# Layer norm rows split into fp16 parts before they are turned, and turned by transposing DMAs instead of TensorE

## The chip, the cores and the metric

One core of one Trainium2 chip runs the whole program. The metric is device time in microseconds (us). Engines are named as in the profile: PE is TensorE (PEld its weight loads), DVE is VectorE, ACT is ScalarE, POOL is GpSimd, SP is SyncE, which here only issues DMAs. PSUM is the memory that TensorE writes; SBUF is the other on-chip memory. The kernel is written by hand for each engine: an engine runs its own list of instructions in order, and waits on semaphores (counters) that others raise.

## The reference

```
x    = x + xattn(layernorm(x), ctx)          # x: 4 x 2048 x 512, ctx: 4 x 77 x 512
xattn: q = n @ Wq.T, k = ctx @ Wk.T, v = ctx @ Wv.T, 16 heads of 32
       a = softmax(mask(q k^T / sqrt(32))) v ;  return a @ Wo.T
x    = x + ffn(layernorm(x))
ffn:   s = n @ Win + bin (512 -> 64);  h = relu(s[..., None] * W1 + b1) (64 x 16)
       g = sum_h(h * W2) + b2 (64);    return g @ Wout + bout (64 -> 512)
```

All inputs are fp32. A product of two fp32 operands is made on TensorE from fp16 parts: each operand is split into a high part (rounded to fp16) and a low part (what is left), and three passes high·high, high·low, low·high are added up in PSUM (`three_passes`).

## The kernel before

The 8192 rows are 16 groups of 512 rows, each of 4 tiles of 128 rows. One step i of the pipeline works on several groups at once: it takes statistics of group i+2 ("ahead"), makes the normed rows and q of group i+1 ("front"), the logits and softmax of group i ("soft"), probabilities times v, the Wo product, the residual and the second norm of group i-1 ("back"), and the FFN of group i-2 ("ffn"). Steps run from -2 to 17; steps 2 to 13 are three rounds of a hardware loop over four steps. In each engine's `one_step` the order of the instructions is written out by hand, and it is that list that the diff rewrites.

A layer norm's output is needed with the 512 features on the partitions. Before: ACT (`x_normal`) or DVE (`h_normal`) writes the normed fp32 rows to `normed` (4 tiles), PE turns a tile by four 128x128 transposes into a bank of `tr_banks` (`x_transpose`, `h_transpose`), ACT copies the bank to the fp16 high part (`x_part`, `h_part`), and DVE subtracts that from the bank to make the low part (`x_low`, `h_low`), which also frees the bank.

The transposes of the probabilities (`p_transposes`, 16 heads, each copied out by ACT in `p_copies`) and the FFN's spreading products (`ffn_pre`, 8, each read by ACT in `relus`) use the same two banks `tr_banks` in turn (`TR_ORDER`): place n+2 waits for the reader of place n. The logits use two banks (`lg_banks`), of which each is freed by the first DVE instruction of `maxima`. A half k of a group's softmax goes PE `logits` -> DVE `maxima` -> POOL `subtract_max` -> ACT `exps` -> DVE `sums` -> POOL `divide`; the eight halves are 4 tiles x 2 halves of the heads. `p_transposes(step, 0)` waits until seven halves are divided, so on `divide(step, 6)`, which is the last instruction of POOL in the step before.

At the end of a step DVE runs, in this order, the statistics of the group ahead, `residual` of the four Wo tiles, the second norm (`h_means`, `h_normal`, `h_low`), with `q_low(3)` in between (the next step's `logits(0)` waits for it), and last `sums(step, 6)`. POOL runs `back_rstd`, `front_rstd`, four `add_bout` and the divisions 4 to 6 there. SP issues the loads of x, the stores of the output and the copies of k, and waits for each in order.

Of the kernel before, what the change touches and what calls it, by code (L numbers as in the profile page):

```python
# [31 lines left out]
F32 = mybir.dt.float32  # L32
F16 = mybir.dt.float16
# [6 lines left out]
P = 128  # L40
# [12 lines left out]
LW = HC * KEYS  # L53
HALVES = 2 * T
# [17 lines left out]
    [(FRONT, "xT", k) for k in range(0, 2)] + [(BACK, "pT", k) for k in range(0, 2)] + [(FFN, "pre", 0)]  # L72
    + [(BACK, "pT", 2)] + [(FFN, "pre", 1)] + [(BACK, "pT", k) for k in range(3, 5)]
    + [(FFN, "pre", k) for k in range(2, 4)] + [(BACK, "pT", 5)] + [(FFN, "pre", k) for k in range(4, 6)]
    + [(BACK, "pT", 6)] + [(FFN, "pre", k) for k in range(6, 8)] + [(BACK, "pT", 7)] + [(FRONT, "xT", 2)]
    + [(LATE, "wvT", k) for k in range(0, 4)] + [(BACK, "pT", k) for k in range(8, 12)] + [(FRONT, "xT", 3)]
    + [(BACK, "pT", k) for k in range(12, 15)] + [(LATE, "woT", k) for k in range(0, 2)] + [(BACK, "pT", 15)]
    + [(LATE, "woT", k) for k in range(2, 4)] + [(BACK, "hT", k) for k in range(0, 4)]
# [46 lines left out]
class Ring:  # L125
# [41 lines left out]

    def wait_all_read(self, eng, step):

        for b in range(2):  # L170
            eng.wait_ge(self.free[b], self.half(step))
# [6 lines left out]
def build(nc, x, ctx_in, mask, Wq, Wk, Wv, Wo, Win, bin_, W1, b1, W2, b2, Wout, bout, out):  # L178
    stack = ExitStack()
    with stack:  # L180
# [41 lines left out]
        pT = sb("pT", [P, 8, ROWS], F32)  # L222
# [18 lines left out]
        wvT = pT[:, 4:8, :]  # L241
# [7 lines left out]
        mask_raw = normed[:, :, 0:T * KEYS].bitcast(I32)  # L249
# [33 lines left out]
        x_high = sem("x_high")  # L283
        q_high = sem("q_high")
# [14 lines left out]
        h_high = sem("h_high")  # L299
        s_high = sem("s_high")  # L300
# [23 lines left out]
        def _(sp):  # L324
# [31 lines left out]


# [18 lines left out]

            sp.wait_ge(wout_high, 1)
# [13 lines left out]
            with sp.Fori(0, LOOPED // 4, 1) as t:  # L391
                for v in range(FIRST_FULL, FIRST_FULL + 4):
                    step = Step(t, v)
                    if v % 2 == 0:
                        sp.wait_ge(lg_ready, HALVES * step.i)
                        keys(0 if v % 4 == 2 else 1, t + 1)
                    for half in range(2):
                        store(step, half)

                        sp.wait_ge(out_stored[step.group(2).slot][half], 16 * step.group(2).lap)  # L400
                        load(step.group(2), (half,))
            for i in range(FIRST_FULL + LOOPED, GROUPS + 2):
                for half in range(2):
                    store(Step(0, i), half)
# [114 lines left out]
        def _(act):  # L519
# [53 lines left out]
            def x_normal(g, t):  # L573

                act.wait_ge(x_shift, g.n + 1)
                act.activation(normed[:, t, :], xr[:, g.slot, t, :], ACT.Identity, scale=rstd[:, 0, t:t + 1],
                               bias=shift[:, t:t + 1]).then_inc(x_norm, 1)

            def x_part(step, t):
                tr.wait_ready(act, step, "xT", t)  # L580
                act.activation(xT[:, 0, :, P * t:P * (t + 1)], tr.bank(step, "xT", t).rearrange(
                    "p (c r) -> p c r", c=C), ACT.Copy).then_inc(x_high, 1)

            def h_part(step, t):
                tr.wait_ready(act, step, "hT", t)
                act.activation(hT[:, 0, :, P * t:P * (t + 1)], tr.bank(step, "hT", t).rearrange(  # L586
                    "p (c r) -> p c r", c=C), ACT.Copy).then_inc(h_high, 1)
# [725 lines left out]
```

## Time and profile before

| | us |
|---|---|
| Three runs of the kernel | 977.37, 977.57, 981.69 (median 977.57) |
| Span of the profiled execution | 976.4 |
| PE busy | 890.4 (91%) |
| DVE busy | 743.7 (76%) |
| ACT busy | 529.9 (54%) |
| POOL busy | 445.5 (46%) |

The span is the profiled execution's own time, from its first to its last instruction. A busy time is the time in which an engine ran at least one instruction. A row of a timeline gives the start, how long the instruction or the run of like instructions lasted, the engine, the line of the kernel, the output and the inputs, and in brackets how long the engine had been idle and for whom it waited. A step begins, for the reading here, where the Wo product (L1054 with `woT`, x48) starts on PE.

### The profile page before, as it was taken

What the parts mean: (1) busy time and instruction counts of PE and PEld (TensorE: products, weight loads), DVE (VectorE), ACT (ScalarE), POOL (GpSimd) and SP (SyncE); (2) the same over time, 40 slices, a digit from 0 to 9 for tenths busy, and PEclk for the clock granted to TensorE, in tenths of its full rate; (3) what the DMA queues carried; (4) which work ended last, traced back from release to release, by engine and by line L of the source; (5) the groups of instructions that cost most, each with busy time, mean ns of one, the idle gap of its engine ahead of it and who ended that gap; (6) DMA issues with size and microseconds to landing.
All of it is one profiled execution on the core that took longest, in us unless ns stands there. A gap on an engine that the chain in (4) does not pass through costs nothing.

```text
span 976.4 us, 15372 instructions
## 1 busy us (share of the span) xinstructions
PE 890.4 (91%) x5202; PEld 478.6 (49%) x5202; DVE 743.7 (76%) x1338; ACT 529.9 (54%) x897; POOL 445.5 (46%) x398
## 2 busy tenths in 40 slices
PE   6878799999999989999999989999999999997866
PEld 4434545454555545454555545454555545453331
DVE  2446888888979796888979786888979798778351
ACT  2334638475574837475574827475574738273622
POOL 4033445364636453364646453364645454455220
PEclk9799899999999999999999999999999999999997
DMA  9300000202020110202020110202020100001001
GB/s 341 96 1 0 13 1 7 88 1 87 7 74 21 61 33 4 87 1 87 7 87 8 65 30 3 87 1 87 7 88 7 66 21 35 10 1 44 4 40 44
DMA packets 23314, 42.77 MB, mean 44 GB/s; under 512 B 11519, under 2 KB 12183, under 8 KB 23231
## 3 DMA queue, kind: packets, MB, share of 16 engines
q1 hardware_dynamic: 22303, 40.44, 12.4%
q10 hardware_dynamic: 928, 1.27, 0.4%
q8 instruction: 46, 0.75, 0.3%
q14 instruction: 37, 0.30, 0.1%
HBM read 22.90 MB, written 16.78 MB: 41 GB/s over the span
## 4 chain that ended last, share of the span: by engine, by line
PE 60%; DVE 18%; issue 9%; ACT 7%; POOL 5%; ACTq 0%; DVEq 0%; POOLq 0%
PE mm_banks L1054 19%; PE tr_banks L1105 12%; PE lg_banks L1094 8%; PE mm_banks L1116 7%; DVE normed L862 4%; PE mm_banks L1159 3%; ACT inner L618 3%; DVE xr L846 3%; PE tr_banks L1063 3%; PE mm_banks L1170 3%; DVE row_sum L833 2%; PE tr_banks L1151 2%; DVE stats L787 2%; ACT pT L603 2%; PE tr_banks L1136 2%
## 5 line engine op out<-in xcount | busy, mean ns | idle before, releaser
L468 POOL TENSOR_TENSOR probs<-probs,row_max 128x616 f32<-128x616 f32 x128 | 154.4, 1217 | 181.8 <-DVE row_max L825 181.0
L475 POOL TENSOR_TENSOR probs<-probs,row_inv 128x616 f32<-128x616 f32 x128 | 156.6, 1224 | 154.9 <-DVE row_inv L835 154.9
L1054 PE MATMUL mm_banks<-xT,wqT 128*128 128x512 f16 x768 | 177.4, 382 | 1.5 <-DVE xT L800 1.5
L1054 PE MATMUL mm_banks<-woT,aT 128*128 128x512 f16 x768 | 168.4, 379 | 2.1 <-issue 2.1
L1105 PE MATMUL tr_banks<-ident,probs 128*77 128x128 f32 x1024 | 155.7, 282 | 15.0 <-ACT inner L618 6.1
L1105 PEld LDWEIGHTS tr_banks<-ident,probs 128*77 128x77 f32 x1024 | 117.5, 148 | 95.1 <-issue 34.5
L603 ACT ACTIVATE pT<-tr_banks 77x512 f32<-77x512 f32 x256 | 145.7, 589 | 20.5 <-PE tr_banks L1105 18.2
L1094 PE MATMUL lg_banks<-k_blocks,qT 128*128 128x308 f16 x768 | 125.2, 300 | 15.4 <-issue 12.6
L833 DVE TENSOR_REDUCE row_sum<-probs 128x8 f32<-128x616 f32 x128 | 100.3, 784 | 46.2 <-ACT probs L598 45.2
L586 ACT ACTIVATE hT<-tr_banks 128x512 f16<-128x512 f32 x64 | 34.8, 594 | 171.5 <-PE tr_banks L1136 171.5
L1054 PEld LDWEIGHTS mm_banks<-woT,aT 128*128 128x128 f16 x768 | 75.1, 98 | 93.3 <-issue 3.2
L1054 PEld LDWEIGHTS mm_banks<-xT,wqT 128*128 128x128 f16 x768 | 75.5, 98 | 81.8 <-issue 3.1
L821 DVE TENSOR_TENSOR probs<-lg_banks,mask_bias 128x616 f32<-128x616 f32 x128 | 101.0, 789 | 9.7 <-PE lg_banks L1094 4.6
L825 DVE TENSOR_REDUCE row_max<-probs 128x8 f32<-128x616 f32 x128 | 101.8, 795 | 4.4
L1094 PEld LDWEIGHTS lg_banks<-k_blocks,qT 128*128 128x128 f16 x768 | 72.3, 99 | 62.8 <-issue 29.3
L618 ACT ACTIVATE inner<-tr_banks,inner_cols,w_div 128x512 f32<-128x512 f32 x128 | 95.5, 772 | 10.9 <-PE tr_banks L1151 10.9
L591 ACT ACTIVATE qT<-mm_banks 128x512 f16<-128x512 f32 x64 | 38.2, 597 | 109.2 <-PE mm_banks L1054 109.2
L598 ACT ACTIVATE probs<-probs 128x616 f32<-128x616 f32 x128 | 90.7, 710 | 5.4 <-POOL probs L468 3.5
L457 POOL TENSOR_TENSOR xr<-xr,bout_rows 128x512 f32<-128x512 f32 x64 | 85.6, 1338 | 9.8 <-DVE normed L862 9.8
L447 POOL TENSOR_TENSOR rstd<-var_eps,neg_half 128x2 f32<-128x2 f32 x32 | 22.6, 708 | 117.5 <-DVE var_eps L857 116.1
L1116 PE MATMUL mm_banks<-pT,v_now 77*32 77x512 f32 x512 | 68.2, 604 | 1.8 <-issue 1.7
L806 DVE TENSOR_TENSOR qT<-mm_banks,qT 128x512 f16<-128x512 f32 x64 | 43.9, 686 | 32.2 <-ACT qT L591 31.7
(80 smaller groups left out, 1055.5 us busy)
## 6 DMA issues: line engine op xcount, KB each, us to landing
xr<-in_x SPq DMA_DIRECT2D x32, 512.0 KB, 4.6
out_x<-xr SPq DMA_DIRECT2D x32, 512.0 KB, 2.8
k_blocks<-kT_all SPq DMA_DIRECT2D x32, 38.5 KB, 2.2
probs<-in_L_xattn_Wk SPq DMA_DIRECT2D x1, 1024.0 KB, 8.7
probs<-in_L_xattn_Wq SPq DMA_DIRECT2D x1, 1024.0 KB, 12.8
probs<-in_L_xattn_Wv SPq DMA_DIRECT2D x1, 1024.0 KB, 14.4
probs<-in_L_xattn_Wo SPq DMA_DIRECT2D x1, 1024.0 KB, 16.2
xr<-in_ctx SPq DMA_DIRECT2D x1, 616.0 KB
```

Source lines behind the costliest of these rows:

```text
L468: pool.tensor_tensor(block_of(g, k), block_of(g, k), top, ALU.subtract).then_inc(shifted, 1)
L475: pool.tensor_tensor(block_of(g, k), block_of(g, k), inv, ALU.mult).then_inc(probs_ready, 1)
L598: act.activation(p, p, ACT.Exp, scale=DK ** -0.5 / W_SCALE).then_inc(exp_done, 1)
L603: tr.read(act.activation(pT[0:KEYS, h % 8, :], tr.bank(step, "pT", h)[0:KEYS, :], ACT.Copy), step, "pT", h)
L618: tr.read(act.activation(inner[:, j, :], tr.bank(step, "pre", j), ACT.Relu, bias=inner_cols[:, 1, j:j + 1], scale=w1_div[:, j:j + 1]), ste ...
L821: dve.tensor_tensor(probs_of(g, k), logits_of(k), mask_bias[:, g.slot, k // 2, :].unsqueeze(1).unsqueeze(1).broadcast_to([P, 2, HC, KEYS]) ...
L825: dve.tensor_reduce(row_max[:, g.parity, k, :, :], probs_of(g, k), AX.X, ALU.max)\
L833: dve.tensor_reduce(row_sum[:, k % 2, :, :], p, AX.X, ALU.add).then_inc(sum_done, 1)
L1054: last = pe.matmul(bank, stationary(a, c), moving(b, c), start=(n == 0), stop=(n == len(passes) - 1))
L1094: last = pe.matmul(bank, qT[:, g.parity, qp, c, rows], k_blocks[:, buffer, kp, c, :], start=(m == 0), stop=(m == 2))
L1105: last = pe.transpose(tr.bank(step, "pT", h)[0:KEYS, P * t:P * (t + 1)], probs[:, g.parity, t, KEYS * h:KEYS * (h + 1)], ident[:, :])
L1116: last = pe.matmul(mm.bank(step, "pv", c)[DK * h:DK * (h + 1), :], v_now[:, DK * (HC * c + h):DK * (HC * c + h + 1)], pT[0:KEYS, (HC * c + ...
```

## The change

The normed rows are split in row layout. `normed` shrinks from four tiles to two, shared in turn by both norms. ACT copies a tile of `normed` to the fp16 high part in a new buffer `parts`, DVE subtracts `parts` from `normed` for the low part, and SP issues one transposing DMA for each tile, which turns both parts at once (8 blocks of 128x128 fp16) from `parts` into `xT` or `hT`. PE no longer turns these rows; `q` and `ffn_in` wait for the DMAs. `parts` has four tiles for both norms: the first norm's tile t of a step is written only when the DMA of the second norm's tile t of the step before has landed, and the other way round. `pT` shrinks from 8 to 6 slots. SP's loop is unrolled.

```diff
-        normed = sb("normed", [P, T, D], F32)
-        xT = sb("xT", [P, 2, C, ROWS], F16)
-        hT = sb("hT", [P, 2, C, ROWS], F16)
+        normed = sb("normed", [P, 2, D], F32)
+        parts = sb("parts", [P, T, 2, D], F16)
+        xT = sb("xT", [P, T, 2, C, P], F16)
+        hT = sb("hT", [P, T, 2, C, P], F16)
...
+            def turn_x(step, t):
+                g = step.group(1)
+                if t == 0 and not step.first(-1):
+                    mm.wait_all_ready(sp, step)
+                sp.wait_ge(x_low_done, 4 * g.n + t + 1)
+                sp.dma_start_transpose(xT[:, t, :, :, :].rearrange("p a c r -> p (a c) r"),
+                                       parts[:, t, :, :].rearrange("p a d -> p (a d)")).then_inc(x_turned[t], 16)
+
+            def turn_h(step, t):
+                g = step.group(-1)
+                if t == 0 and not step.first(1):
+                    mm.wait_ready(sp, step, "s", 0)
+                sp.wait_ge(h_low_done, 4 * g.n + t + 1)
+                sp.dma_start_transpose(hT[:, t, :, :, :].rearrange("p a c r -> p (a c) r"),
+                                       parts[:, t, :, :].rearrange("p a d -> p (a d)")).then_inc(h_turned[t], 16)
...
+                for k in range(T):
+                    turn_x(step, k)
+                for half in range(2):
+                    store(step, half)
+
+                    sp.wait_ge(out_stored[step.group(2).slot][half], 16 * step.group(2).lap)
+                    load(step.group(2), (half,))
+                for k in range(T):
+                    turn_h(step, k)
...
             def x_part(step, t):
-                tr.wait_ready(act, step, "xT", t)
-                act.activation(xT[:, 0, :, P * t:P * (t + 1)], tr.bank(step, "xT", t).rearrange(
-                    "p (c r) -> p c r", c=C), ACT.Copy).then_inc(x_high, 1)
+                g = step.group(1)
+                if not (step.first(-1) or step.first(0) or step.first(1)):
+                    act.wait_ge(h_turned[t], 16 * (g.n - 2))
+                elif not step.first(-1):
+                    act.wait_ge(x_turned[t], 16 * g.n)
+                act.wait_ge(x_norm, 4 * g.n + t + 1)
+                act.activation(parts[:, t, 0, :], normed[:, t % 2, :], ACT.Copy).then_inc(x_high, 1)
...
             def h_low(step, t):
                 dve.wait_ge(h_high, 4 * step.group(-1).n + t + 1)
-                rows = slice(P * t, P * (t + 1))
-                tr.read(dve.tensor_tensor(hT[:, 1, :, rows], tr.bank(step, "hT", t).rearrange("p (c r) -> p c r", c=C),
-                                          hT[:, 0, :, rows], ALU.subtract), step, "hT", t)
+                dve.tensor_tensor(parts[:, t, 1, :], normed[:, t % 2, :], parts[:, t, 0, :], ALU.subtract)\
+                    .then_inc(h_low_done, 1)
...
             def ffn_in(step):
 
-                tr.wait_all_read(pe, step)
+                for t in range(T):
+                    pe.wait_ge(h_turned[t], 16 * (step.group(-2).n + 1))
```

`x_normal` and `h_normal` of tiles 2 and 3 now wait for the low part of tiles 0 and 1 (two tiles of `normed`). On DVE `x_low(2)` and `x_low(3)` move up among the first `maxima`, and `s_low` moves behind `x_low(3)`.

PE, from the end of one step of the loop to the FFN's part of the next, before. L1136 and L1063 are the transposes of the second and the first norm, L1094 the logits, L1105 the probabilities' transposes, L1054 with `hT` is `ffn_in`, L1151 is `ffn_pre`.

```order
L1094 MATMUL lg_banks<-k_blocks,qT 128x308 x6
...
L1136 MATMUL tr_banks<-ident,normed 128x128 x4
...
L1094 MATMUL lg_banks<-k_blocks,qT 128x308 x6
...
L1063 MATMUL tr_banks<-ident,normed 128x128 x4
L1061 REGISTER_ALU
L1063 MATMUL tr_banks<-ident,normed 128x128 x4
L1054 MATMUL mm_banks<-hT,win 128x512 x12
...
L1105 MATMUL tr_banks<-ident,probs 77x128 x8
L1094 MATMUL lg_banks<-k_blocks,qT 128x308 x6
...
L1151 MATMUL tr_banks<-s_parts,spread 128x512
```

The same place of the changed kernel (L1145 logits, L1156 the probabilities' transposes, L1114 with `hT` is `ffn_in`, L1195 is `ffn_pre`):

```order
L1145 MATMUL lg_banks<-k_blocks,qT 128x308 x6
...
L1145 MATMUL lg_banks<-k_blocks,qT 128x308 x6
L1152 REGISTER_ALU
L156 ISA
L1156 MATMUL tr_banks<-ident,probs 77x128 x8
L1145 MATMUL lg_banks<-k_blocks,qT 128x308 x6
...
L1156 MATMUL tr_banks<-ident,probs 77x128 x4
...
L1156 MATMUL tr_banks<-ident,probs 77x128 x4
L1186 REGISTER_ALU
L1114 MATMUL mm_banks<-hT,win 128x512 x12
L165 REGISTER_ALU
L1195 MATMUL tr_banks<-s_parts,spread 128x512
```

The transposes of both norms are gone, the probabilities' transposes stand right behind `logits(0)`, and `ffn_in` stands behind those of head 4, with `ffn_pre(0)` directly after it.

ACT at the start of a step, before (L576 `x_normal`, L581 `x_part`, L612 `s_part`, L603 `p_copies`, L618 `relus`):

```order
L576 ACTIVATE normed<-xr,shift,rstd 128x512 x2
L161 ISA
L581 ACTIVATE xT<-tr_banks 128x4x128
L161 REGISTER_ALU
L581 ACTIVATE xT<-tr_banks 128x4x128
L576 ACTIVATE normed<-xr,shift,rstd 128x512
L161 ISA
L612 ACTIVATE s_parts<-mm_banks,bin 128x512
L161 REGISTER_ALU
L603 ACTIVATE pT<-tr_banks 77x512
```

and now (L626 `x_normal`, L636 `x_part`, L658 `p_copies`, L667 `s_part`):

```order
L626 ACTIVATE normed<-xr,shift,rstd 128x512 x2
L160 ISA
L658 ACTIVATE pT<-tr_banks 77x512
...
L635 REGISTER_ALU
L636 ACTIVATE parts<-normed 128x512
L160 REGISTER_ALU
L658 ACTIVATE pT<-tr_banks 77x512
...
L658 ACTIVATE pT<-tr_banks 77x512
L160 ISA
L667 ACTIVATE s_parts<-mm_banks,bin 128x512
L160 REGISTER_ALU
L673 ACTIVATE inner<-tr_banks,inner_cols,w_div 128x512
```

`s_part`, and with it all eight `relus`, come behind the copies of heads 0 to 4, and two `x_part` stand among these copies.

## Rows read from the trace of the kernel before

**Rows 1.** The page, section 4: shares of the chain that ended last.

```profile
PE 60%; DVE 18%; issue 9%; ACT 7%; POOL 5%; ACTq 0%; DVEq 0%; POOLq 0%
```

**Rows 2.** Busy time by stretch: start:end, length, each engine (x instructions), clock, DMA, GB/s.

```profile
405.47:459.05 53.58, 51.97 (x318) 28.05 (x317) 45.63 (x83) 31.91 (x54) 27.21 (x25) 1.00 0.13 40
405.47:426.72 21.25, 20.47 (x110) 10.69 (x108) 20.18 (x44) 7.86 (x13) 14.33 (x14) 1.00 0.00 0
426.72:441.40 14.68, 13.85 (x100) 8.12 (x100) 11.64 (x17) 12.82 (x21) 4.21 (x4) 1.00 0.01 2
441.40:459.05 17.65, 17.65 (x111) 9.24 (x112) 13.80 (x24) 11.23 (x20) 8.67 (x8) 1.00 0.37 120
```

**Rows 3.** Timeline of PE: start, us, what, [idle before, releaser].

```profile
405.47 10.52 PE L1054 MATMUL mm_banks<-woT,aT 128*128 128x512 f16 x48
...
420.90 1.11 PE L1136 MATMUL tr_banks<-ident,normed 128*128 128x128 f32 x8 [0.65 <-DVE normed L862]
422.13 0.96 PE L1094 MATMUL lg_banks<-k_blocks,qT 128*128 128x308 f16 x6
...
424.13 2.75 PE L1054 MATMUL mm_banks<-hT,win 128*128 128x512 f16 x12
```

**Rows 4.** Groups of instructions, PE: both norms' transposes; busy, mean ns, idle before.

```profile
L1063 PE MATMUL tr_banks<-ident,normed 128*128 128x128 f32 x256 | 41.7, 295 | 3.0 <-ACT normed L576 2.1 <-DVE xT L800 0.6
L1136 PE MATMUL tr_banks<-ident,normed 128*128 128x128 f32 x256 | 34.9, 281 | 17.3 <-DVE normed L862 17.3
```

**Rows 5.** Timeline of DVE in the second norm.

```profile
417.49 0.69 DVE L868 TENSOR_TENSOR hT<-tr_banks,hT 128x512 f16<-128x512 f32 x1
419.36 1.94 DVE L862 TENSOR_SCALAR normed<-xr,mean_var,rstd 128x512 f32<-128x512 f32 x2 [0.23 <-POOL rstd L447]
421.22 0.68 DVE L806 TENSOR_TENSOR qT<-mm_banks,qT 128x512 f16<-128x512 f32 x1
```

**Rows 6.** Timeline of POOL over the same time.

```profile
417.29 1.22 POOL L475 TENSOR_TENSOR probs<-probs,row_inv 128x616 f32<-128x616 f32 x1
...
419.29 1.27 POOL L457 TENSOR_TENSOR xr<-xr,bout_rows 128x512 f32<-128x512 f32 x1
...
424.79 1.22 POOL L475 TENSOR_TENSOR probs<-probs,row_inv 128x616 f32<-128x616 f32 x1
```

**Rows 7.** Timeline of DVE and POOL while FFN weights are split.

```profile
98.13 0.78 DVE L764 SCALAR_TENSOR_TENSOR inner<-inner 64x512 f16<-64x512 f32 x1 [1.05 <-ACT inner L559]
98.33 2.27 POOL L475 TENSOR_TENSOR probs<-probs,row_inv 128x616 f32<-128x616 f32 x1
98.84 0.68 DVE L767 SCALAR_TENSOR_TENSOR win<-inner,win 128x512 f16<-128x512 f32 x1
```

**Rows 8.** Timelines of ACT and DVE at the FFN's first product.

```profile
426.92 0.69 ACT L612 ACTIVATE s_parts<-mm_banks,bin 128x512 f16<-128x512 f32 x1 [1.16 <-PE mm_banks L1054]
...
427.64 0.76 DVE L874 SCALAR_TENSOR_TENSOR s_parts<-mm_banks,bin,s_parts 64x512 f16<-64x512 f32 x1 [0.47 <-ACT s_parts L612]
```

**Rows 9.** Timeline of ACT: two `relus`, one of `exps`, one of `p_copies`.

```profile
434.53 1.43 ACT L618 ACTIVATE inner<-tr_banks,inner_cols,w_div 128x512 f32<-128x512 f32 x2
435.86 0.71 ACT L598 ACTIVATE probs<-probs 128x616 f32<-128x616 f32 x1
436.70 0.59 ACT L603 ACTIVATE pT<-tr_banks 77x512 f32<-77x512 f32 x1
```

**Rows 10.** The page, section 6: DMA issues, KB of each, median us to landing.

```profile
k_blocks<-kT_all SPq DMA_DIRECT2D x32, 38.5 KB, 2.2
...
probs<-in_L_xattn_Wo SPq DMA_DIRECT2D x1, 1024.0 KB, 16.2
```

**Rows 11.** Timeline of PE: the Wo products of steps 5, 15 and 16.

```profile
346.98 10.52 PE L1054 MATMUL mm_banks<-woT,aT 128*128 128x512 f16 x48
...
886.21 10.52 PE L1054 MATMUL mm_banks<-woT,aT 128*128 128x512 f16 x48 [0.58 <-issue]
933.52 10.52 PE L1054 MATMUL mm_banks<-woT,aT 128*128 128x512 f16 x48 [1.48 <-issue]
```

More of the change, by code:

```diff
@@ L166, in wait_read, with wait_all_ready @@
         eng.wait_ge(self.free[place % 2], self.half(step) + place // 2 + 1)
+    def wait_all_ready(self, eng, step):
+        eng.wait_ge(self.ready, 2 * self.half(step))
     def wait_all_read(self, eng, step):
@@ L389, in store @@
                 sp.dma_start(out_rows[g.n][:, tiles, :], xr[:, g.slot, tiles, :]).then_inc(out_stored[g.slot][half], 16)
[L391 to L401, printed above, removed]
+            for k in range(T):
+                turn_x(Step(0, 1), k)
+            for k in range(T):
+                turn_h(Step(0, 1), k)
+            for i in range(FIRST_FULL, FIRST_FULL + LOOPED):
+                step = Step(0, i)
+                if i % 2 == 0:
+                    sp.wait_ge(lg_ready, HALVES * i)
+                    keys(0 if i % 4 == 2 else 1, (i - FIRST_FULL) // 4 + 1)
+                for k in range(T):
+                    turn_x(step, k)
[3 more added lines that the diff above has]
+                    load(step.group(2), (half,))
+                for k in range(T):
+                    turn_h(step, k)
             for i in range(FIRST_FULL + LOOPED, GROUPS + 2):
+                step = Step(0, i)
+                if FRONT in step.parts:
+                    for k in range(T):
+                        turn_x(step, k)
                 for half in range(2):
-                    store(Step(0, i), half)
+                    store(step, half)
+                if BACK in step.parts:
+                    for k in range(T):
+                        turn_h(step, k)
             for s in range(4):
@@ L650, in one_step @@
                 if ffn:
+                    s_part(step)
+                    relus(step, 0)
+                if back:
+                    p_copies(step, 5)
+                if ffn:
+                    relus(step, 1)
                     relus(step, 2)
+                if back:
+                    exps(step, -1)
+                    p_copies(step, 6)
+                if ffn:
                     relus(step, 3)
                 if back:
-                    p_copies(step, 5)
+                    a_part(step, 0)
                 if ffn:
@@ L658, in one_step @@
                 if back:
-                    exps(step, -1)
-                    p_copies(step, 6)
+                    p_copies(step, 7)
                 if ffn:
@@ L663, in one_step @@
                     relus(step, 7)
-                if back:
-                    a_part(step, 0)
-                    p_copies(step, 7)
-                if front:
-                    x_part(step, 2)
                 if late:
@@ L681, in one_step @@
                     p_copies(step, 9, 10, 11)
-                if front:
-                    x_part(step, 3)
                 if late:
@@ L726, in one_step @@
                     q_part(step, 3)
-                if ahead:
-                    x_normal(step.group(2), 0)
                 if back:
@@ L732, in one_step @@
                 if ahead:
+                    x_normal(step.group(2), 0)
                     x_normal(step.group(2), 1)
@@ L902, in one_step @@
                     x_low(step, 1)
+                if soft:
+                    maxima(step, 0)
+                    maxima(step, 1)
+                if front:
+                    x_low(step, 2)
+                if soft:
+                    maxima(step, 2)
+                if front:
+                    x_low(step, 3)
                 if ffn:
@@ L915, in one_step @@
                     a_low(step, 0)
-                if front:
-                    x_low(step, 2)
                 if soft:
@@ L927, in one_step @@
                     output(step, 2)
-                if front:
-                    x_low(step, 3)
                 if ffn:
```

132 lines of the change are left out of this document (57 added, 75 removed).

## The prediction

> **What bounds the kernel now.** I read the shares of the chain first: PE holds 60% of it, DVE, ACT and POOL together 30% [rows 1]. That says PE is the bound with the others close behind, and it is an average, so I cut one step of the loop out. From one first Wo product to the next it takes 53.58 us, PE is busy 51.97 of them and DVE 45.63 [rows 2]. Cut again, the step has three stretches. In the first, 21.25 us from the Wo product to the first transpose of probabilities (call it pT0), DVE is busy 20.18 us and POOL 14.33 us: nearly as full as PE's 20.47. In the second, 14.68 us up to the end of the FFN's g product, ACT is busy 12.82 us. Only the third, 17.65 us, is PE alone (17.65) [rows 2]. So a microsecond taken from PE is worth a microsecond only in the third stretch.
>
> All times in a step below are counted from its Wo product, T = 405.47 in the trace [rows 3].
>
> **What is removed.** The 512 transposes cost PE 41.7 + 34.9 = 76.6 us of busy time and 17.3 + 3.0 us of waits before them, 96.9 us over 16 groups, about 6.1 us a group [rows 4]. Of the 32 transposes of a step, 24 lie in the first stretch, 8 in the other two, at about 0.16 us (41.7/256) each: 1.3 us outside the first stretch.
>
> **First stretch: where the gain goes.** Without the transposes and with `ffn_in` moved behind, PE has four Wo products, q(3) and two logits to do before pT0. Four Wo products end at T+10.4 (10.52 less the overlap), q(3) takes 2.6 as `ffn_in` does (426.72 - 424.13) and each logits 0.9 (423.06 - 422.13 is the slot) [rows 3]: PE is there at T+14.8. But pT0 waits for `divide(step, 6)` on POOL, which runs from 424.79 for 1.22 us, to T+20.5 [rows 6]. Before, pT0 stood at T+21.25, so this chain was hidden by 0.7 us only. It does not go through PE once the Wo products are done: DVE residuals, the POOL and DVE work of the norm, q_low(3) at 421.22 (for which `logits(0)` waits, which began at 422.13 before), then `sums(6)`, then POOL [rows 3, 5, 6]. Nothing of it is shortened. The gain of the first stretch is 0.7 us and PE idles for almost 6.
>
> **The lock, first stretch.** The new `h_low` and `x_low` read two SBUF operands (`normed`, `parts`); the old ones read PSUM and SBUF [rows 5]. The trace has such DVE instructions once: L764 and L767, back to back from 98.13 to 99.5. A POOL division that started at 98.33 took 2.27 us instead of 1.22, so 1.05 us more, about what was left of the two [rows 6, 7]. In the second norm there is the same seen from DVE: `h_normal` x2 starting 0.07 us after an `add_bout` takes 1.94 us [rows 5, 6], where two alone take 1.0. I take it that the new low parts and POOL's big instructions exclude each other. The Trainium skill says the same (SBUF — State Buffer, "Who interferes with whom": a DVE instruction with two SBUF inputs and a GpSimd one that reads SBUF block each other for a whole instruction); the trace agrees with its 2.27 us. Worked through the step: h_low(0), at 417.49, finds the division of 417.29 running [rows 5, 6] and starts some 0.9 us later, and with it the variance of the second pair, its rstd, h_normal(2) and (3). h_low(2) and (3) then hold POOL for another 2 x 0.6. Together +2.0 us on `divide(6)`: pT0 at T+22.6. Bounds: 0 if there is no such lock, 3.1 if POOL keeps it through its run of three instructions and DVE waits for all.
>
> **Second stretch.** ACT must now do, in its order, four `x_normal` and `x_part`, of which `x_normal(2)` and `(3)` wait for `x_low(0)` and `(1)`. I place these: without the lock head 0 is copied at T+22.1, with it at T+24.6, since x_low(0) and (1) stand behind POOL's last division and hold it. Then heads 1, 2 and two `x_part` follow at 0.54 us each, head 4's transposes end at T+27.4, `ffn_in` (2.6) at T+30.0. Here comes a wait that had a cover before: `s_part` 0.69 and `s_low` 0.76 [rows 8], with 0.15 for signals 1.6 us, lay beside pT0, pT1 and logits(1), and now `ffn_pre(0)` stands directly behind `ffn_in`. It starts at T+31.7. From there ACT is the bound: eight `relus` at 0.7, three `p_copies` at 0.54, one `exps` 0.62 and one `a_part` 0.54 (spacings of the rows) are 8.4 us [rows 9], with two banks in turn and PE's own order 9.3 until g can start. g takes 1.9, end at T+42.9. Before it was at 441.40, T+35.9: +7.0.
>
> **Third stretch.** PE alone as before, less one tile of transposes (4 x 0.16, with the overlap 0.44): 17.2. The step is 42.9 + 17.2 = 60.1 us, +6.5.
>
> **The DMAs.** Eight transposing DMAs of 256 KB a step. No row shows one. Below: 2.2 us, the small SBUF copy; above: 16.2 us, the slowest landing shown [rows 10]. I take 3, near the lower row, as plain SBUF traffic of a quarter of the size of the upper row's, whose 16.2 us include others ahead of it. Below even 2.2, nothing changes. With 3 the last `h_low` at T+19 lands at T+23.5 at the latest, `ffn_in` needs it at T+27.4, and `x_part(3)` at T+26.8: hidden, by 3 us. SP has nothing else there: its stores and loads come mid-step, behind four `turn_x` that are ready by T+33 and before any output. From about 5 us apiece the cover is gone (`x_part(3)` waits, and ACT's copies behind it, and PE for them), from 60.1/8 = 7.5 us SP's DMAs bound the step.
>
> **Sum.** Steps 2 to 14 are 13 full ones: 13 x 6.5 = 84.5. Step 15 has no first norm: +7.1 (0 off for x, the rest as above). Step 16 has no softmax of its own, which leaves `ffn_in` moved, s uncovered and part of the lock: +3.0 on 47.3 us [rows 11]. The last step gets the DMA's latency and the lock: +2.7. Three rounds of the loop cost 58.49 - 53.58 = 4.9 us where engines start a new round (346.98 to 405.47, [rows 2, 3, 11]); PE's share now falls into its wait for POOL: -1.7 each, -5.1, estimated from the 4.9 less what DVE alone would lose. The setup: four tiles go through a DMA before the first q, +2.5, and steps 0 and 1 save their transposes, -2.5. Together +92, on a span of 976.4: 1068.6. The median of the runs shown is 1.2 above the span: 1070.
>
> **Rivals.**
> The same without the lock. pT0 at T+20.6, head 0 copied at T+22.1, `ffn_pre(0)` at T+29.3, g ends at T+40.4: 57.6 a step, 13 x 4.05 = 53, end +8.6, rounds -5: 976.4 + 57 + 1.2, about 1034. For it: the evidence for two SBUF inputs is one division. Against: its 1.05 us fits well.
> Only the first wait. If ACT and PE pack the second stretch as tightly as before, `ffn_in` 2.6 and s 1.6 are added, the 6.6 us of the first stretch's transposes and `ffn_in` are lost to the wait: T+20.6 + 16.5 + 17.2 = 54.3 a step, 13 x 0.75 = 10, with the ends 985 to 995. Against it: ACT is busy 12.82 of 14.68 us there already [rows 2].
> Faster. PE stays the bound because POOL's division of the seventh half comes earlier than I think, the DVE queue in front of it being shorter by its waits for PE's transposes. It decides from a division that ends by T+14.8; then 76.6 us of transposes and some of their waits go, less 6 for the setup and the end: about 900. For it: PE is 91% busy. Against: DVE has 20.18 busy of 21.25 us there, only 0.23 us of a wait before h_normal [rows 2, 5].
> The DMAs are slow. At 10 us each SP needs 80 us a step: 13 x 26.4 on top, about 1320; at 6 us some 9 us a step and 1100 to 1190. For it: nothing in the trace; against: the small copy's 2.2 us [rows 10]. The Trainium skill has both answers: 1309 ns for one 128x128 block (VectorE: DVE Perf Modes, "The three transpose paths"), of which a DMA here has eight, and "TRN2 transpose DMAs are as fast as regular DMAs" (Advanced Engine Details and Errata, "X-Bar Transpose (TRN2)"). By the first, if blocks don't overlap, this rival is the outcome, by the second the cover holds; no run here shows it yet.
>
> **How the numbers follow.** The forecast 0.46 (1045 to 1095, by the lock's bounds); no lock 0.23 (1015 to 1045); only the first wait 0.08 (978 to 1000); faster 0.12; slow DMAs 0.11 (from 1100 up). The range 978 to 1125 leaves out the faster case, most of the slow DMAs and a little of the forecast's own tail, 0.2 together. A measurement tells 0.5%, 5 us, from no change: faster 0.12 and a trace of the third case 0.01, within 0.05 from the third case and chance, slower 0.82.
>
> **What would show it.** In the changed profile: PE idle 5 to 8 us a step before L1156 at a step's start, released by POOL's division (right: first stretch); an idle of 1.6 us before L1195, released by DVE `s_parts`; PE's transposes of probabilities and `ffn_pre` waiting for ACT; POOL divisions or `add_bout` of 1.8 us and more, or low parts of 1.2 and more, in the second norm (right: lock; all at 1.2 and 0.69: wrong); transposing DMAs landing in 2 to 4 us. A third stretch much above 17.2 us, or PE waiting for DMAs, would mean that I missed a wait. A step under 53 us means that the first stretch was read wrong.

## The result, and the profile after

| | before | after |
|---|---|---|
| Four runs each, us | 977.37 to 982.52, median 979.63 | 1116.82 to 1122.69, median 1118.88 |
| Span of the profiled execution | 976.4 | 1115.1 |
| PE busy | 890.4 (91%) | 876.9 (79%) |
| DVE busy | 743.7 (76%) | 793.1 (71%) |
| POOL busy | 445.5 (46%) | 476.0 (43%) |

The ratio of times is 1.143, with a 95% interval of 1.140 to 1.146: slower by 139 us. PE's transposes cost 76.6 us before, and PE is busy only 13.5 us less now, in the main because part of what is left runs at a lower clock (below): the logits and the probabilities' transposes alone are busy 40.3 us longer. DVE and POOL are busier by 49.4 and 30.5 us, with the same work. The chain that ended last, by engine, after:

```profile
PE 36%; issue 24%; DVE 19%; POOL 14%; ACT 6%; ACTq 1%; DMA 0%; DVEq 0%; POOLq 0%
```

PE fell from 60% to 36%, DVE and POOL rose from 23% to 33% together, and "issue" from 9% to 24% [rows 1]. DMA has 0%: of the new transfers only one, of 2.79 us in the last step, is on this chain.

One step of the loop, and its three stretches cut at the same instructions as before (columns as in [rows 2]):

```profile
322.36:383.87 61.51, 50.25 (x286) 25.58 (x285) 48.94 (x83) 32.70 (x54) 29.20 (x25) 0.94 0.26 69
322.36:345.16 22.80, 14.86 (x74) 6.88 (x72) 21.68 (x43) 7.00 (x11) 14.91 (x13) 0.92 0.21 49
345.16:366.43 21.27, 17.95 (x106) 9.84 (x106) 14.51 (x21) 14.77 (x24) 5.62 (x4) 0.92 0.24 55
366.43:383.87 17.44, 17.44 (x111) 8.86 (x108) 12.75 (x21) 10.94 (x19) 8.67 (x8) 1.00 0.35 112
```

Against 21.25, 14.68 and 17.65 us the stretches changed by +1.55, +6.59 and -0.21 us. PE, DVE and POOL at the places of [rows 3, 5, 6], T = 322.36:

```profile
335.31 0.95 PE L1145 MATMUL lg_banks<-k_blocks,qT 128*128 128x308 f16 x6
340.27 0.96 PE L1145 MATMUL lg_banks<-k_blocks,qT 128*128 128x308 f16 x6 [4.02 <-DVE qT L859]
345.16 1.98 PE L1156 MATMUL tr_banks<-ident,probs 128*77 128x128 f32 x8 [3.92 <-POOL probs L519]
346.94 1.70 PE L1145 MATMUL lg_banks<-k_blocks,qT 128*128 128x308 f16 x6
...
351.02 2.75 PE L1114 MATMUL mm_banks<-hT,win 128*128 128x512 f16 x12
355.35 0.39 PE L1195 MATMUL tr_banks<-s_parts,spread 128*128 128x512 f16 x1 [1.57 <-DVE s_parts L932]
```

```profile
334.37 1.57 DVE L926 TENSOR_TENSOR parts<-normed,parts 128x512 f16<-128x512 f32 x1
...
337.50 1.94 DVE L921 TENSOR_SCALAR normed<-xr,mean_var,rstd 128x512 f32<-128x512 f32 x2 [0.60 <-POOL rstd L491]
...
339.96 2.77 DVE L926 TENSOR_TENSOR parts<-normed,parts 128x512 f16<-128x512 f32 x2
...
345.12 2.30 DVE L853 TENSOR_TENSOR parts<-normed,parts 128x512 f16<-128x512 f32 x2
```

```profile
334.17 1.22 POOL L519 TENSOR_TENSOR probs<-probs,row_inv 128x616 f32<-128x616 f32 x1
...
336.38 1.08 POOL L491 TENSOR_TENSOR rstd<-var_eps,neg_half 128x2 f32<-128x2 f32 x1 [0.99 <-DVE var_eps L910]
...
340.52 1.66 POOL L519 TENSOR_TENSOR probs<-probs,row_inv 128x616 f32<-128x616 f32 x1
342.14 1.71 POOL L501 TENSOR_TENSOR xr<-xr,bout_rows 128x512 f32<-128x512 f32 x1
343.81 1.21 POOL L519 TENSOR_TENSOR probs<-probs,row_inv 128x616 f32<-128x616 f32 x1
345.28 1.59 POOL L512 TENSOR_TENSOR probs<-probs,row_max 128x616 f32<-128x616 f32 x1 [0.25 <-DVE row_max L878]
```

PE waits for two things in the first stretch, 4.02 us for q_low(3) and 3.92 us for the last division, then 1.57 us for s. The low parts take 1.57, 2.77/2 and 2.30/2 us instead of 0.69, and POOL's instructions that lie beside them 1.59 to 1.71 us instead of 1.22 to 1.27. The low part of 334.37 ends at 335.94, 0.55 us after the division that started at 334.17: it took its own time only when the whole division was over. After PE's waits the first eight transposes of probabilities take 1.98 us, where they took 1.17 before (at 426.72): the granted clock is 0.92 over these stretches, where it was 1.00, and single instructions run at about half speed (the logits of 346.94 take 1.70 us, those of 335.31 0.95), the lower of the two levels (1.2 and 2.4 GHz).

What PE waited for over the whole program (us in total, times, longest), and the landing time of the new DMAs:

```profile
PE tr_banks L1156 <- POOL probs L519: 60.4, 16, 11.1
PE lg_banks L1145 <- DVE qT L859: 49.0, 12, 4.3
PE tr_banks L1195 <- DVE s_parts L932: 25.2, 16, 1.6
...
PE mm_banks L1114 <- DMA xT<-parts: 14.2, 1, 14.2
```

```profile
xT<-parts SPq DMA_TRANSPOSE x64, 2.8
```

### The profile page after: what moved, and what is told of

It is laid out like the page before. It is cut to its first block, busy times and chain, and to the rows that moved or that the text cites. A ratio compares the mean times of both kernels' runs of the same rounds, so it can differ in the third digit from the quotient of the medians.

```text
span 1115.1 us, 14406 instructions
## 1 busy us (share of the span) xinstructions
PE 876.9 (79%) x4690; PEld 443.9 (40%) x4690; DVE 793.1 (71%) x1338; ACT 541.5 (49%) x897; POOL 476.0 (43%) x398
## 3 DMA queue, kind: packets, MB, share of 16 engines
q10 hardware_dynamic: 928, 1.27, 0.3%
## 4 chain that ended last, share of the span: by engine, by line
PE 36%; issue 24%; DVE 19%; POOL 14%; ACT 6%; ACTq 1%; DMA 0%; DVEq 0%; POOLq 0%
PE tr_banks L1156 9%; PE mm_banks L1114 9%; POOL probs L519 6%; PE lg_banks L1145 5%; DVE parts L926 4%; PE mm_banks L1167 4%; DVE parts L853 3%; ACT pT L658 3%; PE mm_banks L1203 3%; POOL probs L512 3%; PE mm_banks L1214 2%; PE tr_banks L1195 2%; POOL rstd L491 2%; DVE normed L921 2%; DVE probs L874 2%
## 5 line engine op out<-in xcount | busy, mean ns | idle before, releaser
L519 POOL TENSOR_TENSOR probs<-probs,row_inv 128x616 f32<-128x616 f32 x128 | 163.2, 1276 | 245.6 <-DVE row_inv L888 245.6
L512 POOL TENSOR_TENSOR probs<-probs,row_max 128x616 f32<-128x616 f32 x128 | 165.3, 1302 | 174.0 <-DVE row_max L878 174.0
L1156 PE MATMUL tr_banks<-ident,probs 128*77 128x128 f32 x1024 | 172.5, 308 | 72.7 <-POOL probs L519 60.4
L1145 PE MATMUL lg_banks<-k_blocks,qT 128*128 128x308 f16 x768 | 148.7, 340 | 70.9 <-DVE qT L859 49.0
L1156 PEld LDWEIGHTS tr_banks<-ident,probs 128*77 128x77 f32 x1024 | 135.1, 166 | 158.8 <-issue 87.5
L1114 PE MATMUL mm_banks<-xT,wqT 128*128 128x512 f16 x768 | 177.7, 382 | 14.2 <-DMA xT<-parts 14.2
L1114 PE MATMUL mm_banks<-woT,aT 128*128 128x512 f16 x768 | 170.0, 382 | 2.1 <-issue 2.1
L658 ACT ACTIVATE pT<-tr_banks 77x512 f32<-77x512 f32 x256 | 144.8, 589 | 42.6 <-PE tr_banks L1156 37.8
L1145 PEld LDWEIGHTS lg_banks<-k_blocks,qT 128*128 128x128 f16 x768 | 81.7, 110 | 126.9 <-issue 78.3
L642 ACT ACTIVATE parts<-normed 128x512 f16<-128x512 f32 x64 | 36.9, 623 | 190.3 <-DVE normed L921 190.3
L1114 PEld LDWEIGHTS mm_banks<-xT,wqT 128*128 128x128 f16 x768 | 75.7, 99 | 97.6 <-issue 17.9
L1114 PEld LDWEIGHTS mm_banks<-woT,aT 128*128 128x128 f16 x768 | 75.4, 98 | 94.7 <-issue 5.4
L501 POOL TENSOR_TENSOR xr<-xr,bout_rows 128x512 f32<-128x512 f32 x64 | 92.4, 1444 | 9.8 <-DVE normed L921 9.8
L1195 PE MATMUL tr_banks<-s_parts,spread 128*128 128x512 f16 x128 | 52.2, 410 | 48.6 <-DVE s_parts L932 25.2
L626 ACT ACTIVATE normed<-xr,shift,rstd 128x512 f32<-128x512 f32 x64 | 51.6, 814 | 66.7 <-DVE parts L853 39.2
```

What stands on the lines that cost most here:

```text
L501: pool.tensor_tensor(h, h, bout_rows[:, :], ALU.add).then_inc(bout_added, 1)
L512: pool.tensor_tensor(block_of(g, k), block_of(g, k), top, ALU.subtract).then_inc(shifted, 1)
L519: pool.tensor_tensor(block_of(g, k), block_of(g, k), inv, ALU.mult).then_inc(probs_ready, 1)
L658: tr.read(act.activation(pT[0:KEYS, h % PT_SLOTS, :], tr.bank(step, "pT", h)[0:KEYS, :], ACT.Copy), step, "pT", h)
L1114: last = pe.matmul(bank, stationary(a, c), moving(b, c), start=(n == 0), stop=(n == len(passes) - 1))
L1145: last = pe.matmul(bank, qT[:, g.parity, qp, c, rows], k_blocks[:, buffer, kp, c, :], start=(m == 0), stop=(m == 2))
```

## The experiments

Times are medians of the runs, with the ratio to the kernel before, run on the same chip (its medians lay between 976.5 and 978.9), and the ratio's 95% interval. A difference to the kernel after is one between the medians of different sets of runs, in which the kernel before moved by 3 us: less than that can't be told from nothing.

**e1 and e12: fewer transposes, nothing else.** From the kernel before, with one of four transposes for each tile (ACT and DVE read the one block four times, so three quarters of the features are left out); e12 adds five products of 512 columns to PE, before the second norm's last tiles.

```diff
-                for c in range(C):
+                for c in range(1):
                     last = pe.transpose(tr.bank(step, "hT", t)[:, P * c:P * (c + 1)], normed[:, t, P * c:P * (c + 1)],
...
                 if back:
+                    filler(step, 5)      # e12 only
                     h_transpose(step, 2)
```

> The kernel before, but PE turns one of the four blocks of each normed tile, and ACT and DVE read that block four times (the other features are left out). 24 of 32 transposes of a step are gone from PE, nothing else changes. Theory (the first stretch of a step is bound by the chain DVE, POOL, so PE time taken from it is worth nothing): 0.7 us of hidden slack before the first transpose of probabilities and some 0.9 us from the tiles turned in the other stretches, 1 to 2 us a step, 950 to 965 us. Rival (PE is the bound): 3/4 of the 96.9 us of transposes and their waits, so about 905 us.

> The kernel before with one of four blocks turned (as in the first run) and 5 matmuls more (1.1 us) in PE's wait before the second norm's tiles 2 and 3. Theory (there PE's idle time cost clock, ffn_in took 4.43 us instead of 2.75, and that gave back what the missing transposes freed): the clock stays at 1.00, the first transpose of probabilities at T+20.6 to T+21, a step 52 to 52.8 us instead of 53.6, in all 952 to 968 us. Rival (the clock did not matter): 974 to 979 us.

e1: 976.42, 0.998 (0.996 to 1.001), no change. e12: 964.47, 0.983 (0.979 to 0.988). PE at the end of the first stretch, e1 and then e12:

```profile
254.44 0.78 PE L1134 MATMUL tr_banks<-ident,normed 128*128 128x128 f32 x2 [1.09 <-DVE normed L860]
...
257.02 4.43 PE L1052 MATMUL mm_banks<-hT,win 128*128 128x512 f16 x12
```

```profile
252.30 0.78 PE L1134 MATMUL tr_banks<-ident,normed 128*128 128x128 f32 x2
...
254.88 2.75 PE L1052 MATMUL mm_banks<-hT,win 128*128 128x512 f16 x12
257.71 1.04 PE L1103 MATMUL tr_banks<-ident,probs 128*77 128x128 f32 x6
```

In e1 PE waits 1.09 us for the norm, `ffn_in` then takes 4.43 us instead of 2.75 (over 3.7 us in 11 of the 16 groups, in e12 in 4, before in 2), and the gain is gone. With PE kept busy in e12, pT0 starts at T+20.84 (T = 236.87), and most steps take 52.5 to 52.8 us. From the first to the last full step, 13 steps in all, e12 takes 695.3 us and the kernel before 706.6: three quarters of the transposes, 24 x 0.16 = 3.8 us of PE a step, are worth 0.9 us a step. So the forecast's reading of the first stretch holds: PE's work there hides beside DVE's and POOL's.

**e5: the new order of the FFN in the kernel before.** The transposes and the banks' reads stay; only the place of `ffn_in`, `ffn_pre`, `s_part`, `s_low` and `relus` is that of the kernel after.

```diff
     [(FRONT, "xT", k) for k in range(0, 2)] + ...
-    + [(BACK, "pT", k) for k in range(0, 2)] + [(FFN, "pre", 0)] + [(BACK, "pT", 2)] + ...
+    + [(BACK, "pT", k) for k in range(0, 5)] + [(FFN, "pre", 0)] + [(BACK, "pT", 5)] + ...
...
                 if ffn:
-                    ffn_pre(step, 2)
+                    ffn_in(step)
+                    ffn_pre(step, 0)
```

> The kernel before with the changed kernel's order of the FFN part and nothing else: transposes of both norms on PE and read from PSUM, but ffn_in behind the transposes of head 4 with ffn_pre 0 right behind it, s_part and the relus behind the copies of heads 0 to 4, s_low behind maxima 2. Theory (the new order costs by itself, because the 1.6 us of s_part and s_low lose their cover and the eight relus start later): the first transpose of probabilities at T+20.6, ffn_pre 0 some 5 us later than in the kernel before, a step 56.5 to 58 us instead of 53.6, in all 1015 to 1040 us. Rival (the order is harmless, the loss comes from the DMAs, the lock and the clock): 975 to 990 us.

1062.75, 1.087 (1.084 to 1.091). This one edit is worth 85 us, 5.2 us in the step shown, which is one of the shorter ones (58.7 to 60.5 without the starts of rounds):

```profile
308.52:367.30 58.78, 52.51 (x318) 28.11 (x317) 45.85 (x83) 32.12 (x54) 27.17 (x25) 1.00 0.12 40
```

PE is busy 52.51 of 58.78 us, with 2.34 us of a wait for DVE's `xT` before pT0 and 1.57 us for s before `ffn_pre(0)`, at T+29.5. The wait for s and the full queue of ACT behind it come with the order, not with the DMAs. The wait for `xT` (32.7 us in all) belongs to e5 alone: it comes where the old transposes meet the new order, and the kernel after has nothing like it. So 85 us are more than the order costs there (32 us, see e10).

**e2, e9, e3: the lock and the clock, in the kernel after.** In e2 the low parts are left out: their place takes an instruction of about the same length that reads one SBUF operand (1.27 us for two, beside 2.77). e3 gives PE 17 products before `logits(0)` and 16 behind it, with the lock in place; e9 is e2 with such products.

```diff
-                dve.tensor_tensor(parts[:, t, 1, :], normed[:, t % 2, :], parts[:, t, 0, :], ALU.subtract)\
+                dve.bn_stats(low_stats[:, t, :], normed[:, t % 2, :])\
                     .then_inc(h_low_done, 1)
```

```diff
+            def filler(step, count):
+                tr.wait_free(pe, step, "pT", 0)
+                for _ in range(count):
+                    pe.matmul(tr.bank(step, "pT", 0), wqT[:, 0, 0, 0:P], wqT[:, 0, 1, :], start=True, stop=True)
```

> The changed kernel, but the low parts are not computed: in their place DVE runs bn_stats over the same 128x512 fp32 tile, one SBUF input, about as long (0.69 us); the low halves of parts stay zero. Everything waits as before. Theory (two SBUF inputs exclude POOL's instructions): POOL's long instructions go back to 1.22 and 1.27 us, the first transpose of probabilities comes at T+20.6 instead of T+22.8, head 0 is copied some 2 to 3 us earlier, a step takes 58.5 to 59.5 us instead of 61.5, in all 1075 to 1090 us. Rival (the long times come from something else, as the order of the instructions): the same time as the changed kernel, 1119 us.

> The changed kernel, with 17 and 16 matmuls more in PE's two waits of the first stretch (before logits 0 and before the first transpose of probabilities), 3.7 and 3.5 us at full clock, into a bank that is written anew afterwards. Theory (PE's idle time costs clock, the transposes and logits after it run at the low level, 1.98 us for 8 transposes instead of 1.07): the granted clock stays at 1.00, the first transposes take 1.1 us, a step loses 1 to 1.5 us, in all 1095 to 1108 us. Rival (the waits after it are set by ACT and DVE, the slow PE is hidden): clock up but time the same, 1115 to 1122 us. A second rival: the matmuls themselves come late and hold up the transposes: over 1125 us.

> The changed kernel without the low parts (bn_stats in their place, as in the run without the lock) and with 15 and 12 matmuls more in PE's two waits of the first stretch (3.2 and 2.6 us). Theory (with the lock gone the slow PE after its waits lies on the path: 4 us of it at half clock, 8 transposes in 1.99 us, logits in 1.7 us): the clock stays at 1.00, a step takes 57.6 to 58.6 us instead of 60.1 without the lock alone, in all 1035 to 1052 us. Rival (the clock is hidden here too): 1062 to 1068 us, as without the lock alone.

e2: 1067.80, 1.093 (1.089 to 1.097), 51 us below the kernel after. e3: 1114.12, 1.139 (1.135 to 1.144), 5 us below, little more than can be told from nothing. e9: 1054.26, 1.077 (1.074 to 1.080), 14 us below e2. A step in e3, then in e9:

```profile
578.37:639.88 61.51, 55.78 (x319) 27.71 (x318) 48.96 (x83) 32.67 (x54) 29.21 (x25) 1.00 0.28 72
```

```profile
492.57:550.39 57.82, 54.32 (x312) 27.25 (x311) 45.51 (x83) 32.33 (x54) 27.13 (x25) 1.00 0.33 76
```

Both have a clock of 1.00, and between them lies the lock alone: 3.7 us a step. Without a busy PE, e2's pT0 is where expected, T+20.64, but its eight transposes take 1.99 us and its steps 58.8 to 60.4 (without the starts of rounds). With the lock in place the clock costs a steady step nothing: e3's step is the 61.51 us of the kernel after to the hundredth. Why, e3's PE shows (T = 323.41):

```profile
346.14 1.10 PE L1161 MATMUL tr_banks<-ident,probs 128*77 128x128 f32 x8 [0.41 <-POOL probs L519]
347.08 0.95 PE L1150 MATMUL lg_banks<-k_blocks,qT 128*128 128x308 f16 x6
349.92 0.66 PE L1161 MATMUL tr_banks<-ident,probs 128*77 128x128 f32 x4 [1.89 <-ACT pT L658]
```

The 1.6 us saved turn into 1.89 us of waiting for ACT, which itself is late: `x_normal(2)` and `(3)` stand before the copy of head 0 and wait for the two `x_low`, 2.30 us.

**e4: half of the cover for s.** `ffn_in` goes before the transposes of heads 3 and 4, and `s_part` before their copies.

```diff
                     logits(step, 2)
+                if ffn:
+                    ffn_in(step)
                 if back:
                     p_transposes(step, 3, 4)
                 if ffn:
-                    ffn_in(step)
                     ffn_pre(step, 0)
```

> The changed kernel, with ffn_in one place earlier on PE, ahead of the transposes of heads 3 and 4, and s_part ahead of their copies on ACT, so that these two heads stand between ffn_in and ffn_pre 0. Theory: 0.9 us of the 1.6 us wait for s gets its cover back and the relus start 0.5 to 1.5 us earlier: a step 0.7 to 1.5 us shorter, 1097 to 1110 us. Rival (the wait for s only moves, as ACT's eight relus and copies bound that stretch): 1115 to 1122 us. If the DMAs of the second norm land too late for the earlier ffn_in, the time goes up.

1108.10, 1.133 (1.129 to 1.138), 11 us below the kernel after. PE's wait for `s_parts` fell from 25.2 to 12.1 us, by 13.1: the uncovered s costs about what the wait says.

**e6: plain DMAs.** The same source and destination, 256 KB, without the turning (the values in `xT` and `hT` are then not turned).

```diff
-                sp.dma_start_transpose(xT[:, t, :, :, :].rearrange("p a c r -> p (a c) r"),
+                sp.dma_start(xT[:, t, :, :, :].rearrange("p a c r -> p (a c r)"),
```

> The changed kernel with plain DMAs of the same 256 KB a tile in place of the transposing ones (the rows are not turned, the products get them as they are). Theory (the DMAs are hidden in the steps of the loop): a step stays at 61.5 us; only the setup gains, since SP issues four transposing DMAs in 7.9 us there and PE waits 14.2 us for them: 1107 to 1115 us. Rival (transposing DMAs cost in the loop, by their landing or by their 135,000 small packets): below 1100 us.

1116.55, 1.142 (1.138 to 1.147): 2 us, which the measurement can't tell from nothing. They land in 2.2 to 2.3 us where the transposing ones take 2.8. That DMAs transpose costs this kernel nothing a step. In the setup the first q, which waits for four of them, starts at 39.11 instead of 40.27, and the Wo product of step 1 at 134.36 instead of 137.40. Only the first 1.2 us can be laid to them: with transposing DMAs that Wo product starts at 134.53 in e2 as well.

**e7 and e8: no loop.** The twelve steps of the loop written out, in the kernel after (e7) and before (e8).

```diff
-            with eng.Fori(0, LOOPED // 4, 1) as t:
-                for v in range(FIRST_FULL, FIRST_FULL + 4):
-                    one_step(Step(t, v))
+            for i in range(FIRST_FULL, FIRST_FULL + LOOPED):
+                one_step(Step((i - FIRST_FULL) // 4, (i - FIRST_FULL) % 4 + FIRST_FULL))
```

> The changed kernel with the hardware loop of PE, DVE, ACT and POOL written out (SP's is written out already). Theory (the start of a round costs 7.8 us here, at three places, because DVE waits 5.8 us for nothing but its instructions): the three steps drop from 69.3 to 61.5 us, 1119 - 23 = 1096 us. Rival (the written out code is fetched as slowly at other places): the same or slower.

> The kernel before with its loop written out on all engines but SP. Theory: the start of a round costs 4.9 us, at three places: 979.6 - 14.7 = 965 us, which would beat both kernels; with the run above it tells how much of the change's loss lies in the starts of rounds (3 x 2.9 = 9 us). Rival: the same or slower, as above.

e7: 1100.59, 1.126 (1.121 to 1.131), 18 us below the kernel after. e8: 967.19, 0.989 (0.985 to 0.994), 9 us below the kernel before, and so the fastest complete kernel of this study; all of the steps that were looped take 53.56 or 53.57 us. A round's start costs more in the kernel after, since DVE, now on the path, is late there by itself (in the kernel before DVE's longest such wait is 2.79 us):

```profile
411.00 0.80 DVE L874 TENSOR_TENSOR probs<-lg_banks,mask_bias 128x616 f32<-128x616 f32 x1 [5.83 <-issue]
```

**e10 and e11: the DMAs with the old order.** e10 is the kernel after with the FFN's order of before; e11 leaves the low parts out too, as e2 does.

> The changed kernel (rows turned by DMA, two SBUF operands in the low parts) with the FFN's order of the kernel before: ffn_in ahead of the first transposes of probabilities, ffn_pre spread among them, s_part ahead of the copies, s_low behind maxima 0. Theory (the later ffn_in is what costs most, more than waiting for the DMAs would): ffn_in starts when the fourth tile has landed, at T+23 to T+24, the first transpose of probabilities at T+26, g ends at T+41 to T+42.5 instead of T+44: a step 58 to 60 us, in all 1070 to 1095 us. Rival (the later ffn_in is needed for the DMAs): ffn_in waits for the DMAs to T+26 or later and the kernel is no faster than the changed one, 1115 us and more.

> The run before with the low parts left out as well (bn_stats in their place), so neither the new order nor the lock. What is left is the exchange itself: transposes by DMA instead of PE. Theory (PE's time in the first stretch is worth nothing and the landing of the DMAs comes a little later than PE's transposes did): ffn_in at T+20.5 to T+21.5, the first transpose of probabilities at T+23.5 instead of T+21.3, a step 54.5 to 56.5 us, in all 995 to 1025 us: no faster than the kernel before. Rival (the exchange gains once its by-products are gone): under 970 us.

e10: 1086.97, 1.110 (1.106 to 1.113). e11: 1050.17, 1.072 (1.068 to 1.075), far above the 995 to 1025 expected. The medians side by side (for scale, before: 979):

| | low parts from two SBUF operands | without |
|---|---|---|
| new order | 1118.9 | 1067.8 |
| old order | 1087.0 | 1050.2 |

The lock costs 51 us in the new order and 37 in the old; the order costs 32 with the lock and 18 without; and 71 us are neither. Most of them show on e11's PE. Here are its largest waits, then the busy times of a step, then PE in the next step, T = 311.91:

```profile
PE mm_banks L1118 <- DMA hT<-parts: 84.3, 16, 11.0
PE lg_banks L1149 <- DVE qT L862: 33.8, 12, 2.9
PE mm_banks L1118 <- DMA xT<-parts: 14.1, 1, 14.1
```

```profile
253.96:311.91 57.95, 49.71 (x285) 24.98 (x284) 45.66 (x83) 32.51 (x54) 27.10 (x25) 0.94 0.33 80
```

```profile
334.92 5.28 PE L1118 MATMUL mm_banks<-hT,win 128*128 128x512 f16 x12 [5.40 <-DMA hT<-parts]
339.99 1.09 PE L1160 MATMUL tr_banks<-ident,probs 128*77 128x128 f32 x8
```

and the chain through it (start, us, what):

```profile
328.33 1.20 DVE low_stats L929 x2
329.53 0.66 SPq L381
330.19 0.04 issue
330.23 4.45 DMA hT<-parts
334.68 0.24 issue
334.92 5.28 PE mm_banks L1118 x12
```

From the end of DVE's last instruction to PE's first product lie 5.4 us of issue, queue and DMA. The old order has no cover for it: `ffn_in` moves from T+18.7 to T+23.0, and runs at the lower clock after the wait (5.28 us instead of 2.75), so that pT0 stands at T+28.1. This step takes 60.37 us, the one before it 57.95. `ffn_in` takes 4.0 to 5.3 us in all 16 groups, some 28 us together above 2.75 each; as e11 was not run with PE kept busy, what the clock has of the 71 us stays open. The new order covers the DMAs and pays with s and ACT's queue; neither order is free.

## Why the prediction was right, and where its size was off

The direction, the place and the mechanism of the likeliest case held; 1070 was 49 us short. The 1118.9 lie inside the whole range (978 to 1125), but above the 1045 to 1095 that the likeliest case itself was given, in the numbers of the slow DMAs, which did not happen. By its own steps:

**First stretch: right.** pT0 was forecast at T+22.6, behind `divide(6)`, with 5 to 8 us of PE idle; it stands at T+22.80 with 4.02 + 3.92 us idle. e12 shows that PE's transposes were hidden there before as well.

**The lock: the mechanism right, part of its size not.** Forecast +2.0 us on pT0, found +2.2 (T+22.80, against T+20.64 in e2 and T+20.58 in e9). What the forecast set too low is the pair of `x_low` behind the last division. It let them delay head 0's copy by 0.5 us beyond pT0's delay. They take 2.30 us beside POOL's `subtract_max`, `x_normal(3)` waits for them, and head 0 is copied at T+25.9, where e9 has it at T+22.2 (514.77):

```profile
348.24 1.06 ACT L658 ACTIVATE pT<-tr_banks 77x512 f32<-77x512 f32 x2
```

So the whole step loses 61.51 - 57.82 = 3.7 us to the lock, not 60.1 - 57.6 = 2.5. ACT has to wait there because `normed` has two tiles; a run with four was not made. The groups of DVE's low parts say it for the program (687 ns each before):

```profile
L926 DVE TENSOR_TENSOR parts<-normed,parts 128x512 f16<-128x512 f32 x64 | 79.4, 1260 | 1.2 <-ACT parts L642 0.6
L853 DVE TENSOR_TENSOR parts<-normed,parts 128x512 f16<-128x512 f32 x64 | 56.6, 906 | 5.6 <-ACT parts L636 5.6
```

The Trainium skill's rule on two SBUF inputs (SBUF — State Buffer, "Who interferes with whom") has an exclusive lock between a DVE instruction with two SBUF inputs and a GpSimd one that reads SBUF. The trace agrees: with e2's stand-in, which reads one SBUF operand, the division at 570.28 takes 1.21 us, where it takes 1.66 us here. The stand-in also writes less, but that is not the cause: the old `h_low` of 417.49 wrote the same 128x512 fp16 to SBUF beside a division, and both took their usual time [rows 5, 6]. One sign that the forecast read for the lock was none of the change's: the pair of `h_normal` takes 1.94 us before, after, and without the low parts (e9, at 506.45).

**Second stretch: the structure right.** `ffn_pre(0)` forecast at T+31.7, found at T+33.0; from there to the end of g forecast 11.2 us, found 366.43 - 355.35 = 11.1. e9, with neither lock nor low clock, has `ffn_pre(0)` at 521.88, T+29.31, where the rival without the lock put it at T+29.3, and a step of 57.82 us against its 57.6. The missing 1.3 us before `ffn_pre(0)` are the `x_low` above: head 0 was forecast at T+24.6 and is copied at T+25.9, and from there to `ffn_pre(0)` it is 7.11 us in the kernel after and in e9 alike.

**Third stretch:** 17.44 against 17.2.

**The DMAs: right.** Forecast 3 us and hidden; 2.8 and hidden (e6). The slow case fell: the Trainium skill's 1309 ns for a 128x128 block (VectorE: DVE Perf Modes, "The three transpose paths") does not add up over a DMA's eight blocks, and the page that has transposing DMAs as fast as regular ones (Advanced Engine Details and Errata, "X-Bar Transpose (TRN2)") is nearer: 2.8 beside 2.2 to 2.3 us, and 1.23 beside 0.46 us of SP's time to issue (medians). What the forecast did not see is how thin the cover is without the new order (e11).

**The sum.** Forecast +92 on the span, measured +138.7. The terms:

| | forecast | measured | what was missed |
|---|---|---|---|
| 13 steps | +84.5 | 13 x 7.93 = +103.1 | `x_low` under the lock |
| 3 rounds of the loop | -5.1 | +9.9 | sign |
| step 15 | +7.1 | +8.6 | |
| step 16 | +3.0 | +8.1 | |
| end | +2.7 | +4.2 | |
| setup | 0 | +4.9 | the first q waits for its DMAs |

Of the 46.7 us missed, 18.6 are the steps' and 15.0 the rounds'. **The rounds had the wrong sign:** "PE's share now falls into its wait for POOL: -1.7 each". A round's start costs 69.29 - 61.51 = 7.8 us after and cost 4.9 before [rows 2, 3, 11]. It shows at two places, not at three: the first round begins without a delay (its step takes 61.94 us, 53.65 before). The +9.9 are all that the 13 steps take beyond 13 steady ones, 20.0 us after and 10.1 before. I had taken the idle of PE as slack; but the start of a round delays DVE, which is now the path. e7 takes the loop away and gains 18 us, e8 in the kernel before 9; in the 13 steps of the traces it is 16.6 and 10.2 us, so 6.4 of the 9.9 are the loop's, and the rest is steps of up to 62.7 us that e7 has as well. Of the setup's 4.9 us 4.0 are the first q, which waits 14.2 us and starts at 40.27 (36.29 before), behind four DMAs whose issue lasts from 30.56 to 38.43. This term is soft: the first q starts between 33.4 and 36.3 in the runs with the old transposes, and between 40.3 and 42.9 in those with transposing DMAs. The low clock, which the forecast left out, is worth 14 us without the lock (e9) and 5 us with it (e3), outside the steady steps: the interval called step 15 takes 53.7 us there instead of 55.6.

Of step 16's +8.1 about half is the lock: the interval takes 55.37 us after, 51.24 in e2 without the low parts, and 47.31 before.

One rival had a slip in its sum. "Only the first wait" adds 2.6 and 1.6 us to a second stretch of 14.68, which is 18.9 us (18.4 less a tile of transposes), not 16.5: its step would have been some 56.5 us instead of 54.3, its time about 1020 instead of 985 to 995. It did not happen either way: the second stretch takes 21.27 us.

## What to carry to other kernels

A nearly full engine is the bound only in the stretches where no other chain ends later: before taking work from PE, cut a step at the instructions that wait for other engines, and see who is late there. Moving a norm's turning from PE to DMAs also moved DVE's operands from PSUM to SBUF and took the cover from a chain of small steps; the first cost 37 to 51 us, and most of the rest came with the second, or with the exposed DMAs in its place, while three quarters of PE's 77 us of transposes were worth some 15 us (e12). A transposing DMA stands between the last writer and the first reader, with 3.1 us in the last step of the kernel after and 5.4 us where four follow each other (e11), and wants that much other work there.

## What the runs showed that I had not expected

- A wait of 1 us on PE could give back all that was gained: after the wait of 1.09 us in e1, `ffn_in` took 4.43 us instead of 2.75 (granted clock 0.92 over the stretch of 22.28 us), and 24 transposes left out a step gave no time. Five products a step that nothing reads gave 12 us back (e12).
- The lock reaches small instructions of POOL: `rstd` on 128x2 took 1.08 us beside a low part, 0.71 without.
- A round of a hardware loop, other than the first, starts at a price, 4.9 us here where PE was the path and 7.8 where DVE was; written out, the kernel before gains 1.1% (e8).
